# Routing steps ahead of gating on VectorE, and rows and identity scaling of the shared path on ScalarE, in a fused cross-attention and mixture-of-experts kernel

## The chip, the cores and the metric

The kernel runs on one core of a Trainium2 chip. It is one launch. The metric is device time in microseconds; the median of three runs of the kernel before is 1365.5 us (1364.32 to 1367.94).

The core has five engines with a queue each. PE is TensorE (matmul), DVE is VectorE, ACT is ScalarE, POOL is GpSimd, SP is the sync engine, which here only issues DMAs. Every engine works its own list in order and waits for the others by semaphores. An instruction that waits therefore holds up everything behind it on its engine.

## The reference

The input x has 16 batches of 256 rows of 256 numbers. First comes gated cross-attention, then a gated feed-forward part with routed experts and a shared path:

```python
x = x + tanh(g_xattn) * xattn(ctx, layernorm(x), ...)      # 16 heads of 64, keys and values from [ctx; x]
x = x + tanh(g_ffn) * ffn(layernorm(x), ...)

# ffn, h = layernorm(x), flat = its 4096 rows
probs = softmax(flat @ router_w + router_bias)             # 16 choices
top_w, top_i = top_k(probs, 2); norm_w = top_w / (sum(top_w) + 1e-6)
combine = sum(one_hot(top_i) * norm_w)
routed = combine[:, 15] * flat                             # the 16th choice is the identity
for e in range(15):
    routed += combine[:, e] * (silu(flat @ gate_w[e]) * (flat @ up_w[e]) @ down_w[e])
gate = conv1d(h, conv_w, kernel 3, causal)
shared = silu(gate) * (h @ shared_up_w) @ shared_down_w
return shared + routed
```

## The kernel before, in words

x lies in SBUF as X, 32 tiles of 128 rows (two tiles a batch). The program has three stretches.

**Attention** is a software pipeline of 128 steps (16 batches times 8 pairs of heads) with a loop in its middle. Some work belongs to step n but is done a fixed number of steps later, the lag. The routing of a batch is spread over such lags: after the attention of batch j is added to X, `route_vector` and its siblings do STATS (lag 13, mean and variance of the rows), ROWS (16, normalized rows into h_send), TURN (17 and 18, two transposes on PE), LOGITS (19), PICK (22, the two best choices), RANK (22, matmuls that count how many earlier rows chose each expert), PAGES (23), SLOTS (26, the slot number of each row, then a scatter of the rows to `slots_x` in DRAM by POOL) and SECOND (27, the same for the second choice; it rewrites h_send, so it waits until the first scatter has landed). The last batch is j = 15, so routing goes on for 20 steps after step 127. They are numbered N to N+19, with N = 128. A step N+k does whatever has the right lag there: SLOTS of batch 14 is at N+10, STATS, PICK, PAGES, SLOTS and SECOND of batch 15 are at N+5, N+14, N+15, N+18 and N+19.

**Between attention and the tiles** these 20 steps are mixed with the shared path of batches 0 to 8. `plan()` writes the order by hand, and every engine follows the same list, each doing its own part of an item. Item `("shared", i)` is: DVE makes the normalized rows of batch i+1 (`rows`, into h_row, two instructions); PE transposes the rows of batch i (below T(i)), does the convolution and the up matmul of batch i-1 and the down matmul of batch i-2; ACT copies the transposed rows to hT and takes silu of batch i-1 (act_sh). Item `("gate", i)` is DVE alone: the product gated of batch i-1, then for batch i-2 the identity scaling X = X * x_mul + x_add (two instructions), then the addition of the down result to X (two instructions). In the text, "block i" is PE's part of `("shared", i)`, and gated(m), scaling(m), adding(m) are DVE's parts for batch m. Item `("weights", ...)` turns the logits into the weights of the choices, for tiles 0 to 27 at i = 2 and for the last four after i = 8; it makes x_mul and x_add, and ACT supplies exponentials in its middle.

**The tiles**: 80 tiles of 128 rows, one expert each, are loaded from `slots_x`, and PE, ACT and DVE work on four of them at once (transpose, gate and up matmul, silu, product, transpose, down matmul, scatter by POOL). The first load waits for all scatters. The shared path of batches 9 to 15 goes on there: a block after every eighth tile, its gate after the tile that follows. From tile 26 on the results are gathered back and added to X ("sum"), and stored.

PE waits for gated(m-1) before the convolution of batch m, since both use the PSUM bank pgs, and for adding(m-1) before the down matmul of batch m. The tile's copy xT on DVE frees the PSUM area into which PE puts the next tile's transpose.

What the names are in the rows: `pj<-ident,h_row` (L483) is T(i), `pj<-hT,w_cv` and `pj<-hT,w_su` (L493, L496) convolution and up, `yb<-w_sd,gated` (L507) down; `ov<-seen,all_ones` (L994) is RANK; `ov<-ident,h_send` (L979) is TURN; `h_send<-choice` (L890) is the first instruction of SLOTS, `h_send<-h_send` (L904) of SECOND.

Of the kernel before, what the change touches and what calls it, by code (L numbers as in the profile page):

```python
# [89 lines left out]
def routing_state(nc, keep, s):  # L90
# [3 lines left out]
    def sb(name, shape, dt=F32):  # L94
        return keep.enter_context(nc.sbuf_tensor(name, shape, dt))

    def sem(name):
# [17 lines left out]
        w_top=sb("w_top", [P, NT, 2]), w_id=sb("w_id", [P, NT, 2]), x_mul=sb("x_mul", [P, NT]), x_add=sb("x_add", [P, NT]),  # L115
# [4 lines left out]
def experts(nc, c, X, ident, tanh_g, kept, att, gate_w, up_w, down_w, slots_x, routed_y, out, s):  # L120
# [78 lines left out]
    def plan():  # L199

        steps = list(range(att.N, att.last_step + 1))
        goes_along = (1, 1, 2, 1, 2, 2, 3, 4, 4)
        items = []
        for i in range(EARLY):
            for _ in range(goes_along[i]):
                items.append(("attend", steps.pop(0)))
            if i == 2:
                items.append(("weights", slice(0, WEIGHED)))
            items += [("shared", i), ("gate", i)]
        assert not steps  # L210
        items.append(("weights", slice(WEIGHED, NT)))
# [101 lines left out]
    def scalar(act, attend):  # L313
        parts = [0]

        def shared(i):
# [9 lines left out]
            if on[1]:  # L326
# [35 lines left out]
    def vector(dve, attend):  # L362
# [8 lines left out]
        def rows(b):  # L371
            if b >= 2:
                dve.wait_ge(t_full, b - 1)
            if b >= B - 2:
                dve.wait_ge(att.h_rows, b + 1)
            for t in range(QT):
                n = QT * b + t
                last = ts(h_row[:, b % 2, t, :], X[:, n, :], kept.h_mv[:, n, 0:1], kept.h_rstd[:, n:n + 1],
                          ALU.subtract, ALU.mult)
            last.then_inc(h_ready, 1)  # L380

        def shared(i):
            if i == 0:
                dve.wait_ge(att.h_rows, B - 2)
                rows(0)
            if i + 1 < B:
                rows(i + 1)

        def gate(i):
# [1097 lines left out]
```

## Time and profile before

| | |
|---|---|
| median of three runs | 1365.5 us |
| the profiled execution | 1364.59 us, of which the span of its instructions is 1362.8 us |
| PE busy | 1257.7 us, 92% |
| DVE busy | 900.1 us, 66% |
| POOL busy | 738.3 us, 54% |
| ACT busy | 636.2 us, 47% |
| granted PE clock, mean | 0.981 of full speed |

All times inside the execution are counted from the start of the span. Shares are averages: PE at 92% says that attention and most of the tiles keep it busy, and in the row of 40 slices the places where it isn't stand out. Slices 31 to 33 of PE read 8, 8, 6 (each slice is 34 us), and these hold the stretch between attention and the tiles. A line of the timeline gives the start, the duration of the group, the engine, the line of the kernel, the operation, what is written and read, the shapes and the count, and in brackets how long the engine idled before and who released it.

### The profile page before, as it was taken

The page shows a single profiled execution, that of the slowest core. Times are in us where ns is not written, and L with a number is a line of the kernel's source. Part 1 is how long each engine was busy: PE and PEld are TensorE (multiplying, and loading weights), DVE is VectorE, ACT ScalarE, POOL GpSimd, SP SyncE. Part 2 cuts the span into 40 slices and gives each one's busy share as a digit, 9 for nine tenths or more (in the row PEclk, how much of TensorE's full clock was granted, in tenths as well). Part 3 has the DMA queues.
Part 4 walks back from the last instruction along what each step waited for, and adds up shares of the span by engine and source line. Part 5 has one row for each costly group of instructions (what it writes and reads, how often), then busy time and mean ns, then how long its engine had stood idle before and what let it go on. Part 6 is the DMA issues. An engine that isn't in the chain of part 4 may idle for free. (4 is left out here: it accounts for less than half of the span.)

```text
span 1362.8 us, 28186 instructions
## 1 busy us (share of the span) xinstructions
PE 1257.7 (92%) x8982; PEld 1023.9 (75%) x8982; DVE 900.1 (66%) x2710; ACT 636.2 (47%) x1958; POOL 738.3 (54%) x894
## 2 busy tenths in 40 slices
PE   1899999999999999999999999999999886999996
PEld 1688888878787877778778878788888774877764
DVE  4566677776776777676767676777666564455464
ACT  2555555454554454555454545554555421333332
POOL 1655645666555666566565646565656412454444
PEclk9999999999999999999999999999999987999998
DMA  4950000000000000000000000000000601345656
GB/s 129 296 161 4 3 1 4 17 4 17 7 13 13 9 11 10 12 9 15 7 19 2 19 3 20 1 19 1 17 2 17 182 8 49 112 126 163 201 175 201
DMA packets 61823, 70.90 MB, mean 52 GB/s; under 512 B 7056, under 2 KB 56160, under 8 KB 61664
## 3 DMA queue, kind: packets, MB, share of 16 engines
q1 hardware_dynamic: 54464, 49.96, 12.7%
q0 software_dynamic: 6912, 18.95, 3.8%
q8 instruction: 84, 1.38, 0.4%
q14 instruction: 75, 0.61, 0.1%
q10 hardware_dynamic: 288, 0.00, 0.0%
HBM read 35.19 MB, written 33.70 MB: 51 GB/s over the span
## 5 line engine op out<-in xcount | busy, mean ns | idle before, releaser
L1087 POOL TENSOR_SCALAR probs<-probs,inv_sum 128x333 f32<-128x333 f32 x384 | 425.4, 1123 | 0.0
L1137 ACT ACTIVATE probs<-st,neg_max 128x333 f32<-128x333 f32 x512 | 268.8, 538 | 270.8 <-DVE neg_max L1276 270.8
L1084 POOL TENSOR_TENSOR probs<-probs,inv_sum 128x333 f32<-128x333 f32 x128 | 94.7, 740 | 403.4 <-DVE inv_sum L1287 403.1
L1276 DVE TENSOR_REDUCE neg_max<-st 128x2 f32<-128x666 f32 x256 | 205.9, 846 | 133.1 <-PE st L1369 133.1
L1353 PE MATMUL st<-ident,probs 128*128 128x128 f32 (+1 forms) x1536 | 204.1, 273 | 1.1 <-POOL probs L1087 1.1
L1388 PE MATMUL ov<-PT,V 128*64 128x256 f32 (+1 forms) x1536 | 197.5, 392 | 0.0
L1353 PEld LDWEIGHTS st<-ident,probs 128*128 128x128 f32 (+1 forms) x1536 | 182.8, 143 | 17.9 <-POOL probs L1087 1.4
L1323 PE MATMUL pj<-wkv,lT 128*128 128x512 f32 (+1 forms) x576 | 158.5, 411 | 16.1 <-DVE Q_hl L1296 15.9
L1369 PE MATMUL st<-K_hl,Q_hl 64*128 64x334 f32 x1536 | 153.1, 331 | 18.3 <-issue 8.9
L1308 DVE COPY PT<-st 128x512 f32<-128x512 f32 x256 | 163.8, 682 | 0.8 <-PE st L1353 0.8
L1388 PEld LDWEIGHTS ov<-PT,V 128*64 128x64 f32 (+1 forms) x1536 | 100.2, 138 | 64.7 <-issue 28.5
L1369 PEld LDWEIGHTS st<-K_hl,Q_hl 64*128 64x128 f32 x1536 | 118.8, 187 | 38.9 <-issue 23.4
L1163 ACT ACTIVATE V<-pj 128x512 f32<-128x512 f32 (+1 forms) x96 | 57.2, 596 | 194.1 <-PE pj L1323 194.1
L1323 PE MATMUL pj<-lT,wkv 128*128 128x334 f32 x768 | 140.5, 318 | 2.3 <-DVE wkv L1252 2.3
L1323 PEld LDWEIGHTS pj<-lT,wq 128*128 128x128 f32 x768 | 99.6, 190 | 53.4 <-issue 49.0
L1323 PEld LDWEIGHTS pj<-wkv,lT 128*128 128x128 f32 (+1 forms) x576 | 93.6, 175 | 50.3 <-DVE Q_hl L1296 18.7
L1323 PE MATMUL pj<-lT,wq 128*128 128x256 f32 x768 | 126.7, 300 | 4.1 <-DVE lT L1237 4.1
L1449 PE MATMUL yb<-wo,OT_hl 128*128 128x256 f32 x768 | 122.3, 295 | 0.5 <-DVE OT_hl L1291 0.5
L1323 PEld LDWEIGHTS pj<-lT,wkv 128*128 128x128 f32 x768 | 119.2, 190 | 2.6 <-DVE wkv L1252 2.6
L1137 ACT ACTIVATION_READ_ACCUMULATOR probs<-st,neg_max 128x1 f32 x512 | 103.8, 203 | 1.7 <-issue 1.6
L1449 PEld LDWEIGHTS yb<-wo,OT_hl 128*128 128x128 f32 x768 | 99.3, 190 | 0.8 <-DVE OT_hl L1291 0.8
L1168 ACT ACTIVATE PT<-st 77x512 f32<-77x512 f32 x128 | 75.1, 587 | 29.8 <-PE st L1353 29.8
(175 smaller groups left out, 1729.6 us busy)
## 6 DMA issues: line engine op xcount, KB each, us to landing
slots_x<-zeros SPq DMA_DIRECT2D x10, 1032.0 KB, 13.5
V<-slots_x SPq DMA_DIRECT2D x80, 129.0 KB
yg<-routed_y SPq DMA_DIRECT2D x32, 256.0 KB, 3.2
out<-X SPq DMA_DIRECT2D x32, 128.0 KB
stage<-in_L_xattn_Wkv SPq DMA_DIRECT2D x4, 512.0 KB, 4.0
X<-in_x SPq DMA_DIRECT2D x2, 1024.0 KB, 13.9
w_gu<-in_L_ffn_expert_gate_w SPq DMA_DIRECT2D x2, 960.0 KB, 9.3
w_gu<-in_L_ffn_expert_up_w SPq DMA_DIRECT2D x2, 960.0 KB, 10.3
```

The lines of the kernel that those rows point to most:

```text
L1084: pool.tensor_tensor(probs[:, v, 0, 0:SKV], probs[:, v, 0, 0:SKV], inv_sum[:, v, 0:1].to_broadcast([P, SKV]), ALU.mult).then_inc(normed, 1)
L1087: pool.tensor_scalar(probs[:, v, i, 0:SKV], probs[:, v, i, 0:SKV], inv_sum[:, v, i:i + 1], None, ALU.mult).then_inc(normed, 1)
L1137: nc.scalar.activation(probs[:, v, i, 0:SKV], st_bank(i)[:, 0:SKV], ACT.Exp, bias=neg_max[:, v, i:i + 1], accum_out=sums[:, v, i:i + 1]).t ...
L1163: copy(V[0:kn, kt, half * 512:(half + 1) * 512], bank[0:kn, :], ACT.Copy).then_inc(free, 1)
L1168: copy(PT[0:kn, v, 2, :], st_bank(2)[0:kn, :], ACT.Copy).then_inc(pt_hi, 1)
L1276: nc.vector.tensor_reduce(neg_max[:, v, 2 * i:2 * i + 2], st[i][:, :, 0:SKV], AX.X, ALU.max, negate=True).then_inc(maxed, 1)
L1308: nc.vector.tensor_copy(PT[:, v, kt, :], st_bank(kt)).then_inc(pt_lo, 1)
L1323: last = mm(out, lhs(a, k), rhs(r, k), start=(k == 0 and i == 0), stop=(k == KD - 1 and i == 2))
L1353: last = nc.tensor.transpose(st_bank(kt)[0:kn, at:at + P], probs[:, v, i, k0:k0 + kn], ident[:])
L1369: last = mm(st_bank(2 * qt + head)[:, 0:SKVE], Q_hl[own, r, a, qt * P:(qt + 1) * P], K_hl[own, r, a_, :], start=(n == 0), stop=(n == 2))
L1388: last = mm(ov[half * HALF:(half + 1) * HALF, 0:SQ], V[0:kn, kt, head * DH:(head + 1) * DH], PT[0:kn, v, kt, half * SQ:(half + 1) * SQ], s ...
L1449: last = mm(yb[:, t * D:(t + 1) * D], OT_hl[:, v, a, t * P:(t + 1) * P], wo[:, r_, q, :], start=(q == 0 and t == 0 and i == 0), stop=(q == ...
```

## The change

Three things change.

1. The order in `plan()`. Before, at each i, a few attention steps came first and then `("shared", i), ("gate", i)`. Now the steps from N+4 on stand between `shared` and `gate` of the same i, so that DVE does them before gated; and they are spread otherwise, so that step N+19 comes at i = 7 and no longer at i = 8. The DVE's reads of PE's results (LOGITS and RANK, now items `("reads", n)`) come after the gate. The second `weights` comes at i = 7, ahead of block 8.
2. The rows of the shared path are made by ACT, as Identity with a scale and a bias (h_rstd and the new h_shift = -mean * rstd, which DVE makes in two instructions in all).
3. The identity scaling is made by ACT, after act_sh in `("shared", i)`. The adding on DVE waits for it by the semaphore `scaled`. The chain that makes x_mul and x_add is one dependent step shorter.

```diff
     def plan():
-        steps = list(range(att.N, att.last_step + 1))
-        goes_along = (1, 1, 2, 1, 2, 2, 3, 4, 4)
+        N = att.N
+        before = {0: [N], 1: [N + 1], 2: [N + 2, N + 3]}
+        during = {2: range(N + 4, N + 7), 3: range(N + 7, N + 10), 4: range(N + 10, N + 14), 5: [N + 14],
+                  6: range(N + 15, N + 19), 7: [N + 19]}
+        reads = {2: [N + 6], 4: [N + 11], 5: [N + 14]}
         items = []
         for i in range(EARLY):
-            for _ in range(goes_along[i]):
-                items.append(("attend", steps.pop(0)))
+            items += [("attend", n) for n in before.get(i, ())]
             if i == 2:
-                items.append(("weights", slice(0, WEIGHED)))
-            items += [("shared", i), ("gate", i)]
-        items.append(("weights", slice(WEIGHED, NT)))
+                items += [("reads", N + 3), ("weights", slice(0, WEIGHED))]
+            items.append(("shared", i))
+            items += [("attend", n) for n in during.get(i, ())]
+            items.append(("gate", i))
+            items += [("reads", n) for n in reads.get(i, ())]
+            if i == 7:
+                items.append(("weights", slice(WEIGHED, NT)))
...
     def scalar(act, attend):
+        def rows(b):
+            if b >= 2:
+                act.wait_ge(t_full, b - 1)
+            act.wait_ge(shift_ready, 1 if QT * b < WEIGHED else 2)
+            for t in range(QT):
+                n = QT * b + t
+                last = nc.scalar.activation(h_row[:, b % 2, t, :], X[:, n, :], ACT.Identity,
+                                            bias=h_shift[:, n:n + 1], scale=kept.h_rstd[:, n:n + 1])
+            last.then_inc(h_ready, 1)
         def shared(i):
+            if i == 0:
+                rows(0)
+            if i + 1 < B:
+                rows(i + 1)
...
+            if on[2]:
+                m = i - 2
+                act.wait_ge(mul_ready, 1 if QT * m < WEIGHED else 2)
+                for t in range(QT):
+                    n = QT * m + t
+                    last = nc.scalar.activation(X[:, n, :], X[:, n, :], ACT.Identity,
+                                                bias=x_add[:, n:n + 1], scale=x_mul[:, n:n + 1])
+                last.then_inc(scaled, 1)
...
     def vector(dve, attend):
-        def rows(b):
-            ...
-                last = ts(h_row[:, b % 2, t, :], X[:, n, :], kept.h_mv[:, n, 0:1], kept.h_rstd[:, n:n + 1],
-                          ALU.subtract, ALU.mult)
+        def shift(tl):
+            dve.wait_ge(att.h_rows, tl.stop // QT)
+            dve.wait_ge(att.y_read, tl.stop // QT)
+            nc.vector.scalar_tensor_tensor(h_shift[:, tl], kept.h_mv[:, tl, 0], -1.0, kept.h_rstd[:, tl],
+                                           ALU.mult, ALU.mult).then_inc(shift_ready, 1)
         def gate(i):
...
                 m = i - 2
-                for t in range(QT):
-                    n = QT * m + t
-                    last = ts(X[:, n, :], X[:, n, :], x_mul[:, n:n + 1], x_add[:, n:n + 1], ALU.mult, ALU.add)
-                last.then_inc(scaled, 1)
                 dve.wait_ge(down_full, m + 1)
                 dve.wait_ge(scaled, m + 1)
...
         def weights(tl):
+            if tl.start:
+                shift(tl)
...
-            then(tt(x_add[:, tl], x_add[:, tl], kept.h_rstd[:, tl], ALU.mult))
-            ts(x_mul[:, tl], x_add[:, tl], 1.0, None, ALU.add)
-            then(tt(x_add[:, tl], x_add[:, tl], kept.h_mv[:, tl, 0], ALU.mult))
-            then(ts(x_add[:, tl], x_add[:, tl], -1.0, None, ALU.mult))
+            then(nc.vector.tensor_tensor(x_mul[:, tl], x_add[:, tl], kept.h_rstd[:, tl], ALU.mult))
+            tt(x_add[:, tl], x_add[:, tl], h_shift[:, tl], ALU.mult)
+            ts(x_mul[:, tl], x_mul[:, tl], 1.0, None, ALU.add).then_inc(mul_ready, 1)
```

How the instructions stand on their engines, at three places. The first is DVE behind the first `weights` (i = 2). Before:

```order
L435 TENSOR_SCALAR x_add<-x_add 128x28
L378 TENSOR_SCALAR h_row<-X,h_mv,h_rstd 128x256 x2
L396 TENSOR_TENSOR gated<-pj,act_sh 128x256
L401 TENSOR_SCALAR X<-X,x_mul,x_add 128x256 x2
L407 SCALAR_TENSOR_TENSOR X<-yb,tanh_g,X 128x256 x2
L378 TENSOR_SCALAR h_row<-X,h_mv,h_rstd 128x256 x2
L396 TENSOR_TENSOR gated<-pj,act_sh 128x256
L401 TENSOR_SCALAR X<-X,x_mul,x_add 128x256 x2
L407 SCALAR_TENSOR_TENSOR X<-yb,tanh_g,X 128x256 x2
L820 MEMSET route_carrier 128x1
L829 BN_STATS h_stats<-X 128x6 x2
```

And in the changed kernel, where STATS of batch 15 and PICK of batch 14 follow the weights at once:

```order
L455 TENSOR_SCALAR x_mul<-x_mul 128x28
L840 MEMSET route_carrier 128x1
L849 BN_STATS h_stats<-X 128x6 x2
L840 MEMSET route_carrier 128x1
L853 BN_AGGR h_now<-h_stats 128x2 x2
L840 MEMSET route_carrier 128x1
L875 MAX top<-logit 128x8 x2
```

Two gates stood before STATS and now none does; gated(1) comes eleven rows further down, after PICK. On PE the matmuls of RANK moved likewise, from behind block 3 to behind block 2.

The second place is DVE at SLOTS of batch 15. Before, it came after the gate of i = 7, at i = 8:

```order
L884 TENSOR_TENSOR place<-ranks,room 128x32
L378 TENSOR_SCALAR h_row<-X,h_mv,h_rstd 128x256 x2
L396 TENSOR_TENSOR gated<-pj,act_sh 128x256
L401 TENSOR_SCALAR X<-X,x_mul,x_add 128x256 x2
L407 SCALAR_TENSOR_TENSOR X<-yb,tanh_g,X 128x256 x2
L890 TENSOR_SCALAR h_send<-choice 128x2
L891 TENSOR_TENSOR place<-place,grown 128x32
```

And in the changed kernel, at i = 6:

```order
L904 TENSOR_TENSOR place<-ranks,room 128x32
L910 TENSOR_SCALAR h_send<-choice 128x2
L911 TENSOR_TENSOR place<-place,grown 128x32
L912 TENSOR_TENSOR place<-place,ranks 128x32
L913 TENSOR_TENSOR place<-place,base 128x32
L914 TENSOR_TENSOR placed<-hot,place 128x64
L915 TENSOR_REDUCE slot_f<-placed 128x4
L916 CAST slot_i<-slot_f 128x4
```

SLOTS follows PAGES (which ends with `place<-ranks,room`) without a gate between them, and the gate of i = 6 comes behind SLOTS.

The third place is ACT around the second exponentials. Before, they were its last work ahead of the tiles:

```order
L324 ACTIVATE hT<-pj 128x2x256
L331 ACTIVATE act_sh<-pj 128x256
L336 ACT_TABLE_LOAD
L336 ACTIVATE ex<-ex 128x64
L337 ACTIVATE e<-e 128x4
L346 ACT_TABLE_LOAD
L346 ACTIVATE act_e<-st 128x128 x2
```

And in the changed kernel:

```order
L360 ACTIVATE X<-X,x_add,x_mul 128x256 x2
L367 ACT_TABLE_LOAD
L367 ACTIVATE ex<-ex 128x64
L368 ACTIVATE e<-e 128x4
L331 ACTIVATE h_row<-X,h_shift,h_rstd 128x256 x2
L347 ACTIVATE hT<-pj 128x2x256
L354 ACT_TABLE_LOAD
L354 ACTIVATE act_sh<-pj 128x256
L360 ACTIVATE X<-X,x_add,x_mul 128x256 x2
L377 ACTIVATE act_e<-st 128x128 x2
```

A whole `shared` item, with the rows, the copy to hT, the reload of the silu table, act_sh and the scaling, now stands between the exponentials and the first tile's silu.

## Rows read from the trace of the kernel before

**Rows 1.** From attention's end to the first tile: stretch, length, busy PE, PEld, DVE, ACT, POOL, clock.
```profile
1073.19:1155.78 82.59, 61.41 (x276) 50.59 (x277) 44.24 (x196) 18.58 (x33) 17.11 (x23) 0.80 0.24 71
```

**Rows 2.** Timeline of DVE, from the end of the first weights to the first tile.
```profile
1095.93 0.74 DVE L378 TENSOR_SCALAR h_row<-X,h_mv,h_rstd 128x256 f32<-128x256 f32 x2
...
1103.79 0.42 DVE L829 BATCH_NORM_STATS2 h_stats<-X 128x6 f32<-128x256 f32 x1
...
1114.77 0.42 DVE L396 TENSOR_TENSOR gated<-pj,act_sh 128x256 f32<-128x256 f32 x1 [5.59 <-ACT act_sh L331]
...
1134.15 0.21 DVE L920 COPY ranks<-ov 128x48 f32<-128x48 f32 x1 [1.45 <-PE ov L998]
...
1136.04 0.73 DVE L378 TENSOR_SCALAR h_row<-X,h_mv,h_rstd 128x256 f32<-128x256 f32 x2
...
1143.30 0.16 DVE L890 TENSOR_SCALAR h_send<-choice 128x2 int32<-128x2 f32 x1
...
1148.97 0.17 DVE L904 TENSOR_SCALAR h_send<-h_send 128x2 f32<-128x2 f32 x1 [3.88 <-DMA slots_x<-h_send,slot_i]
...
1151.73 0.15 DVE L419 TENSOR_TENSOR e<-best 128x4 f32<-128x4 f32 x1
...
1156.55 0.42 DVE L443 COPY xT<-st 128x256 f32<-128x256 f32 x1 [1.60 <-PE st L530]
```

**Rows 3.** Timeline of PE in the same stretch.
```profile
1097.30 0.60 PE L483 MATMUL pj<-ident,h_row 128*128 128x128 f32 x4
...
1106.82 0.64 PE L994 MATMUL ov<-seen,all_ones 128*128 128x32 f32 x2 [4.60 <-DVE seen L869]
...
1108.13 1.09 PE L483 MATMUL pj<-ident,h_row 128*128 128x128 f32 x4
...
1115.02 0.60 PE L483 MATMUL pj<-ident,h_row 128*128 128x128 f32 x4
...
1119.78 0.38 PE L979 MATMUL ov<-ident,h_send 128*128 128x128 f32 x2
1120.63 0.44 PE L979 MATMUL ov<-ident,h_send 128*128 128x128 f32 x2 [0.47 <-ACT h_turned L967]
...
1122.46 0.93 PE L483 MATMUL pj<-ident,h_row 128*128 128x128 f32 x4
...
1155.78 0.66 PE L530 MATMUL st<-ident,V 128*128 128x128 f32 x2 [9.29 <-DMA V<-slots_x]
```

**Rows 4.** Busy time in stretches of 5 us; the number after POOL is PE's clock.
```profile
1105.00:1110.00 5.00, 3.18 (x13) 3.00 (x14) 2.41 (x16) 0.60 (x1) 0.82 (x2) 0.56 0.01 3
...
1115.00:1120.00 5.00, 5.00 (x27) 4.32 (x25) 4.64 (x22) 0.98 (x2) 0.00 (x0) 1.00 0.01 2
```

**Rows 5.** Timeline of ACT: copy to hT, table load, exponential of the last tiles.
```profile
1142.21 0.60 ACT L324 ACTIVATE hT<-pj 128x512 f32<-128x512 f32 x1 [0.92 <-PE pj L483]
...
1146.07 1.28 ACT L336 ACT_TABLE_LOAD   x1
1152.05 0.26 ACT L336 ACTIVATE ex<-ex 128x64 f32<-128x64 f32 x1 [4.70 <-DVE ex L420]
```

**Rows 6.** Groups of ACT by shape, first 60 us: a source in SBUF.
```profile
L1125 ACT ACTIVATE wkv<-stage 128x1024 fp32r<-128x1024 f32 x4 | 4.2, 1056 | 13.8 <-DMA stage<-in_L_xattn_Wkv 13.8
```

**Rows 7.** Timeline of all engines around a gate among the tiles.
```profile
1173.16 0.38 ACT L331 ACTIVATE act_sh<-pj 128x256 f32<-128x256 f32 x1 [2.86 <-PE pj L496]
...
1175.11 0.28 ACT L346 ACTIVATE act_e<-st 128x128 f32<-128x128 f32 x1 [1.56 <-PE st L540]
...
1175.96 0.72 DVE L401 TENSOR_SCALAR X<-X,x_mul,x_add 128x256 f32<-128x256 f32 x2
...
1176.79 0.88 DVE L407 SCALAR_TENSOR_TENSOR X<-yb,tanh_g,X 128x256 f32<-128x256 f32 x2
...
1177.58 0.41 DVE L443 COPY xT<-st 128x256 f32<-128x256 f32 x1
...
1178.14 0.41 PE L530 MATMUL st<-ident,V 128*128 128x128 f32 x2 [0.90 <-DVE xT L443]
```

**Rows 8.** Who waited for whom among the tiles: us in total, times, longest.
```profile
PE st L530 <- DVE xT L443: 13.0, 22, 0.9
```

More of the change, by code:

```diff
@@ L114, in routing_state @@
         z_sum=sb("z_sum", [P, NT]), e2=sb("e2", [P, NT]), den=sb("den", [P, NT]),
-        w_top=sb("w_top", [P, NT, 2]), w_id=sb("w_id", [P, NT, 2]), x_mul=sb("x_mul", [P, NT]), x_add=sb("x_add", [P, NT]),
+        w_top=sb("w_top", [P, NT, 2]), w_id=sb("w_id", [P, NT, 2]), x_mul=sb("x_mul", [P, NT]), x_add=sb("x_add", [P, NT]), h_shift=sb("h_shift", [P, NT]),
         conv_in=sem("conv_in"), misc_in=sem("misc_in"), route_consts=sem("route_consts"), cv_ready=sem("cv_ready"),
@@ L156, in experts @@
     x_add = kept.x_add
+    h_shift = kept.h_shift
     pts, pgs, pys = att.pj[0], att.pj[1], att.yb
@@ L175, in experts @@
     scaled = sem("scaled")
+    shift_ready = sem("shift_ready")
+    mul_ready = sem("mul_ready")
     carried = sem("carried")
@@ L199, in plan @@
     def plan():
-        steps = list(range(att.N, att.last_step + 1))
-        goes_along = (1, 1, 2, 1, 2, 2, 3, 4, 4)
+        N = att.N
[3 more added lines that the diff above has]
+        reads = {2: [N + 6], 4: [N + 11], 5: [N + 14]}
         items = []
         for i in range(EARLY):
-            for _ in range(goes_along[i]):
-                items.append(("attend", steps.pop(0)))
+            items += [("attend", n) for n in before.get(i, ())]
             if i == 2:
-                items.append(("weights", slice(0, WEIGHED)))
-            items += [("shared", i), ("gate", i)]
-        assert not steps
-        items.append(("weights", slice(WEIGHED, NT)))
+                items += [("reads", N + 3), ("weights", slice(0, WEIGHED))]
[5 more added lines that the diff above has]
+                items.append(("weights", slice(WEIGHED, NT)))
+        assert att.last_step == N + 19
         shared = EARLY
@@ L369, in then @@
             dve.wait_ge(weigh, steps[0])
-        def rows(b):
[L372 to L375, printed above, removed]
-            for t in range(QT):
-                n = QT * b + t
-                last = ts(h_row[:, b % 2, t, :], X[:, n, :], kept.h_mv[:, n, 0:1], kept.h_rstd[:, n:n + 1],
-                          ALU.subtract, ALU.mult)
-            last.then_inc(h_ready, 1)
         def shared(i):
             if i == 0:
[L384 to L387, printed above, removed]
+                shift(slice(0, WEIGHED))
+        def shift(tl):
[3 more added lines that the diff above has]
+                                           ALU.mult, ALU.mult).then_inc(shift_ready, 1)
         def gate(i):
@@ L398, in gate @@
                 m = i - 2
-                for t in range(QT):
-                    n = QT * m + t
-                    last = ts(X[:, n, :], X[:, n, :], x_mul[:, n:n + 1], x_add[:, n:n + 1], ALU.mult, ALU.add)
-                last.then_inc(scaled, 1)
                 dve.wait_ge(down_full, m + 1)
@@ L466, in combine @@
                 add(t, 1).then_inc(final, 1)
-        follow(attend, {"shared": shared, "gate": gate, "weights": weights, "tile": tile, "sum": combine})
+        follow(attend, {"shared": shared, "gate": gate, "weights": weights, "reads": lambda n: att.vector_reads(dve, n), "tile": tile, "sum": combine})
     def tensor(pe, attend):
@@ L1311, in step @@
                 split_rows(bb, u // PAIRS + 1, L_STEPS[p], (u // PAIRS + 1) % 2)
-            route_vector_reads(dve, bb, u, has)
+            if has(0):
+                route_vector_reads(dve, bb, u, has)
         return pipeline(dve, step)
```

5 lines of the change are left out of this document (4 added, 1 removed).

## The prediction

> **What bounds the kernel now.** I read the slices of busy time first (where is PE not full), then the chain that ended last, then busy time by stretch, and last the timelines of single engines where the chain leaves PE.
>
> The change touches nothing before the end of attention, at 1073.2. From there to the first tile's matmul at 1155.78 PE is busy 61.4 of 82.6 us at a mean clock of 0.80 [rows 1]. PE sat idle 9.29 us before it, for a load of rows that wait for the last scatter [rows 3]. So routing of batch 15 ends the stretch. The reader is to see that routing is slow only because of its place in DVE's queue: DVE waits 5.59 us for act_sh in one gate [rows 2], with routing steps queued behind. RANK waits for PICK that way and PE idles 4.60 us [rows 3], after which its clock is at 0.56, against 1.00 further on [rows 4]. These two are its levels, 1.2 GHz and 2.4 GHz (0.56 mixes them). A block (transpose, convolution, up, down) takes 1108.13 to 1115.02 = 6.9 us mostly at the lower one and 1115.02 to 1119.78 = 4.76 us at the higher one [rows 3].
>
> Among the tiles PE waits for xT 22 times, 13.0 us in all, at most 0.9 [rows 8]. One 0.90 stands behind a gate on DVE: gated, scaling, adding, then xT [rows 7].
>
> **The stretch before the tiles, walked through with the new order.** Attention's tail stays. The first rows are now made by ACT behind one h_shift on DVE. An ACT instruction of 128x256 takes 0.38 [rows 7], and one of 1024 columns out of SBUF 1.056 [rows 6], so source SBUF is no dearer; I take 0.8 for a pair. DVE's pair takes 0.74 or a little more [rows 2], so T(0) starts within 0.3 of before. I count 0.
>
> *i = 2.* The weights end at 1095.93 [rows 2]; one dependent step less, so 1095.7. STATS and PICK come next at once: 1103.79 to RANK at 1106.82 = 3.03 [rows 2, 3]. RANK starts at 1098.75. PE was ready at 1097.30 (where T(3) starts now), so it idles 1.4. RANK takes 1106.82 to 1108.13 = 1.3 [rows 3]: T(3) at 1100.05, later than before by 2.75, paid here for what follows.
>
> *i = 3.* PE idled, so I take the lower clock: block 3 ends at 1106.95. gated can start 0.25 before a block ends (1114.77 against 1115.02) [rows 2, 3]. Then ACT scales (0.8), the adding waits for that and takes 0.8 (1176.79 to 1177.58) [rows 7]: DVE is free 1.35 after a block's end, at 1108.3. PAGES and ROWS ran before in its wait for act_sh, which hides them.
>
> *i = 4.* SLOTS to SECOND took 1143.30 to 1148.97 = 5.67, most of it the scatter [rows 2]: SECOND of batch 14 at 1113.95. It stands before gated(3) now. That is an added wait: behind it are gated(3), on which the convolution in block 5 waits, and adding(2). PE meanwhile has one transpose of TURN (0.4), block 4 at the higher clock (to 1112.15), then the other transpose and LOGITS, 1120.63 to 1122.46 = 1.8 [rows 3], so T(5) at 1113.95 and its convolution at 1114.7. gated(3) ends at 1114.5. The scatter is just hidden; each us more would cost one.
>
> *i = 5, 6.* Block 5 follows a small gap and tiny matmuls; I take 6.9 again: 1120.85. RANK 1.3: T(6) at 1122.15. DVE is free at 1122.2, PAGES 1134.15 to 1136.04 = 1.9 [rows 2], SLOTS of batch 15 at 1124.1 instead of 1143.30, SECOND at 1129.75 instead of 1148.97. From SECOND to the first tile was 6.81 [rows 2, 3]: 1136.55 is when the data allows a tile.
>
> *i = 6 to 8.* Three blocks at the higher clock from 1122.15: 1126.9, 1131.7, 1136.45. PE and data thus arrive together, and what is late next is DVE and ACT. The last adding of i = 7 ends at 1133.05, h_shift and the differences are ready at 1133.55 (0.2 for one, an estimate by the 1.9 of PAGES' nine instructions; 0.3 for the other, 1151.73 to 1152.05 [rows 2, 5]), two exponentials 0.4, rows 0.8, the copy to hT 0.6, the silu table 1.28 [rows 5]: act_sh(7) at 1136.65, 0.85 later than PE would allow. gated 0.4 [rows 2], scaling 0.8, adding 0.8: xT of tile 0 at 1138.65. It was at 1156.55 [rows 2]. **Gain 17.9 us.**
>
> What follows a table load is the least known price here: the row shows 1.28 for the load itself [rows 5] and nothing queued directly behind it. The page "ScalarE: Activation LUTs" of the Trainium skill, section "What ACT_TABLE_LOAD costs", says that a switch costs about 1.38 us of drain on top, which speaks against this change. By that rule the gain of this stretch would be 16.5 in place of 17.9; my sum goes by the row.
>
> **The tiles.** DVE loses two things. The rows cost nothing before, since DVE made them while PE was in the block; on ACT they lie beside the block too. The scaling did cost: adding started 1176.79 - 1175.96 = 0.83 later through it, xT with it, and PE idled 0.90 for xT [rows 7]. Now ACT has act_sh at 1173.16 to 1173.54, the scaling to 1174.35, and its next work, act_e, can't start before 1175.11 [rows 7]. So it is hidden, and done 1.6 before DVE came to the scaling (1175.96) [rows 7]; `scaled` isn't waited for. If this cover went, each gate would cost up to 0.8. PE's idle falls from 0.90 to 0.07, and the next limit is PE's own order. I take 0.8 for each of 8 gates (those of batches 7 to 14 for the scaling) and 0.5 for the last, which has less PE work beside it: **6.9 us**. Bounds: 0, if something else is late at once, and 0.83 x 9 = 7.5.
>
> **Sum.** 17.9 + 6.9 = 24.8. The profiled execution took 1364.59 (span 1362.8), so 1339.8. The median stands 0.9 above that execution: **1340.7 us**.
>
> **Bounds of the walk.** The clock decides most. A block at the other level is 2.1 away: if blocks 3 and 5 both ran at the higher one, 4.2 less; if 6 and 7 also ran at the lower one, 4.2 more. The wait for the scatter in front of gating was seen as 5.67. ACT's pair may cost 0.76 to 1.1 (0.38 twice, or 1.056 for one long instruction): up to 0.3 at each of some five places on the path, 1.5. The likeliest case's own range is thus 1335 to 1346.
>
> **Rivals.**
> 1. *The clock stays up.* The idle of 1.4 before RANK is short against the 4.60 that stood there. For: the smaller gap. Against: the row of TURN shows idle of only 0.47 and still 0.93 for T(6) behind it, against 0.60 at the higher clock [rows 3]. The walk is 4.2 shorter, and the tiles start at most 1.5 faster: 1335 to 1336.
> 2. *Work behind the silu table starts late.* Before, each load had idle time behind it; now act_sh(7) is queued behind one and on the path. If the start is late by as much again as the load is long, 1.3 more: 1342.0. For: the trace can't exclude it; against: no row shows it. That is the mechanism of the rule above.
> 3. *The path moves to ACT and its handoffs.* Every gate waits for act_sh and then for the scaling, and T and the convolution wait for rows and hT from the same queue. If PE loses 0.8, one pair, at each of blocks 3 to 8: 4.8 more, 1345.5. Against: rows are made a block ahead.
> 4. *The tiles gain nothing*, since PE then waits for another: 6.9 more, 1347.6. For: the 13 other waits for xT, (13.0 - 9 x 0.9) / 13 = 0.4 each [rows 8], stand where DVE is busy without a gate; against: the idle of 0.90 behind a gate names DVE as releaser [rows 7].
> 5. *The other side: SECOND in front of gating.* Scatters that landed late would stall DVE at i = 4 and i = 7, and with it gated, PE and the clock. Up to 5.7 us from SLOTS to SECOND it is hidden. Every us beyond costs one in each of the two places, and a block at the lower clock 2.1 each. The change is slower than before once 2 x (t - 5.7) + 4.2 exceeds 24.8, that is, when t is over 16 us. At t = 20 the time is 1340.7 + 28.6 + 4.2 = 1373.5. Against: 5.67 measured, and the queues are nearly empty there (DMA share 0.01 in the stretches shown [rows 4]).
> 6. *The change doesn't shorten routing*, if DVE, not its waits, were the limit: then only the tiles gain, 1358.6. Against: DVE is busy 44.2 of 82.6 us [rows 1].
>
> **How the numbers follow.** Chances: my forecast 0.42, rival 1 0.16, rival 2 0.12, rival 3 0.11, rival 4 0.10, rival 5 0.03, rival 6 0.03, and 0.03 that all evens out to within what can be told. This kernel's measurement tells 0.3%, about 4 us, from no change. All cases but the fifth and the last lie below 1361.4, so faster 0.94, same 0.03, slower 0.03. The range for 8 in 10 takes in the forecast's own range, rival 1, and rivals 2 to 4 with a margin for a clock that falls once more: 1332 to 1351.
>
> **What would show it.** In the profile of the changed kernel: idle of PE before the first tile falls from 9.29 to about 1; the first tile's xT stands at 1137 to 1140; SLOTS of batch 15 at 1124, SECOND 5.7 later, with gated behind it; PE idles about 1.4 before the first RANK between attention and tiles, and under 0.5 before the second; DVE is idle for ACT before each adding by 0.3 to 0.5 ahead of the tiles, and not at all among them; the 0.90 waits for xT behind a gate shrink to 0.1. Wrong would be: a first tile later than 1145 (then rival 3, 5 or 6, told apart by who releases gated), waits for xT as long as before (rival 4), act_sh more than 1 us behind the silu table (rival 2), or idle of PE for gated.

## The result, and the profile after

On one chip, four runs of each: before 1366.42 us, after 1343.83 us (1342.28 to 1344.31), ratio 0.983, 95% interval 0.982 to 0.985. That is faster by 22.6 us, where 24.8 were forecast; 1340.7 was predicted, so the median is 3.1 above the forecast and within the range. Another set of runs with the same kernel, told below, gave the same ratio.

The profiled execution took 1342.28 us (span 1340.5). Busy time from attention's end to the first tile's matmul, in the columns of [rows 1], and two stretches of 5 us as in [rows 4]:

```profile
1074.17:1139.84 65.67, 55.05 (x276) 45.62 (x277) 31.40 (x161) 34.62 (x67) 16.81 (x23) 0.90 0.31 90
1100.00:1105.00 5.00, 5.00 (x17) 4.40 (x18) 3.47 (x18) 0.60 (x1) 0.00 (x0) 0.50 0.02 3
...
1115.00:1120.00 5.00, 4.45 (x17) 3.61 (x17) 3.25 (x22) 0.98 (x2) 2.13 (x3) 0.66 0.18 63
```

The stretch is 65.67 us long, not 82.59. PE had 276 instructions before and has 276 now, but they take 55.05 instead of 61.41 us, for the mean clock is 0.90 instead of 0.80. So 6.4 us of the 16.9 are busy time, at the same count of matmuls and a higher clock, and 10.6 are idle time that went. DVE has 35 instructions less, ACT 34 more. In the second row the clock (0.50) is at the lower of its two levels (1.2 GHz), in the third (0.66) it is so for part of the time.

PE in the same stretch, as in [rows 3]. T is the group L503, a block's convolution L513:

```profile
1073.06 0.97 PE L1470 MATMUL yb<-wo,OT_hl 128*128 128x256 f32 x6 [0.53 <-DVE OT_hl L1311]
...
1090.90 2.76 PE L513 MATMUL pj<-hT,w_cv 128*128 128x256 f32 x12
...
1099.85 0.64 PE L1014 MATMUL ov<-seen,all_ones 128*128 128x32 f32 x2 [4.47 <-DVE seen L889]
...
1101.15 1.09 PE L503 MATMUL pj<-ident,h_row 128*128 128x128 f32 x4
1102.04 4.86 PE L513 MATMUL pj<-hT,w_cv 128*128 128x256 f32 x12
...
1114.46 1.06 PE L1007 MATMUL ov<-w_rt,h_turned 128*128 128x16 f32 x8 [0.64 <-issue]
1115.37 0.63 PE L503 MATMUL pj<-ident,h_row 128*128 128x128 f32 x4
1116.56 4.50 PE L513 MATMUL pj<-hT,w_cv 128*128 128x256 f32 x12 [0.55 <-DVE gated L419]
...
1123.21 0.64 PE L503 MATMUL pj<-ident,h_row 128*128 128x128 f32 x4
...
1139.84 0.41 PE L550 MATMUL st<-ident,V 128*128 128x128 f32 x2 [2.01 <-DMA V<-slots_x]
```

Idle in front of the first tile fell from 9.29 [rows 3] to 2.01, still for the load of rows behind the last scatter. The same twelve convolution matmuls take 2.76 where the granted clock is 1.00 (the one at 1090.90), 4.50 where it is 0.61 on average and 4.86 where it is 0.56, that is, where part of the group ran at the lower level.

DVE, as in [rows 2]. L419 is gated, L426 the adding, L910 the first instruction of SLOTS, L924 the first of SECOND; the line of POOL is the issue of the first of the two scatters of batch 15:

```profile
1108.22 0.42 DVE L419 TENSOR_TENSOR gated<-pj,act_sh 128x256 f32<-128x256 f32 x1 [4.02 <-ACT act_sh L354]
...
1109.28 0.88 DVE L426 SCALAR_TENSOR_TENSOR X<-yb,tanh_g,X 128x256 f32<-128x256 f32 x2 [0.63 <-ACT X L360]
1110.07 0.16 DVE L910 TENSOR_SCALAR h_send<-choice 128x2 int32<-128x2 f32 x1
1115.85 0.17 DVE L924 TENSOR_SCALAR h_send<-h_send 128x2 f32<-128x2 f32 x1 [3.99 <-DMA slots_x<-h_send,slot_i]
1116.00 0.42 DVE L419 TENSOR_TENSOR gated<-pj,act_sh 128x256 f32<-128x256 f32 x1
...
1122.37 0.42 DVE L419 TENSOR_TENSOR gated<-pj,act_sh 128x256 f32<-128x256 f32 x1 [3.01 <-ACT act_sh L354]
...
1126.09 0.17 DVE L910 TENSOR_SCALAR h_send<-choice 128x2 int32<-128x2 f32 x1
...
1127.95 0.98 POOL L977 DMA_INDIRECT slots_x<-h_send,slot_i  x1 [0.15 <-POOL pool_route L975]
...
1132.57 0.17 DVE L924 TENSOR_SCALAR h_send<-h_send 128x2 f32<-128x2 f32 x1 [2.88 <-DMA slots_x<-h_send,slot_i]
...
1138.44 0.42 DVE L419 TENSOR_TENSOR gated<-pj,act_sh 128x256 f32<-128x256 f32 x1 [0.83 <-ACT act_sh L354]
1139.50 0.88 DVE L426 SCALAR_TENSOR_TENSOR X<-yb,tanh_g,X 128x256 f32<-128x256 f32 x2 [0.63 <-ACT X L360]
1140.29 0.42 DVE L463 COPY xT<-st 128x256 f32<-128x256 f32 x1
```

SLOTS of batch 15 stands at 1126.09, where it was at 1143.30 [rows 2]: routing did go ahead of gating. Of the waits for act_sh, 4.02 is left ahead of gated(2), 3.01 ahead of gated(4) and 0.83 ahead of gated(7). SECOND waits 3.99 for the scatter with gated(3) behind it, and PE then waits 0.55 for that gated. At the end both paths meet: xT starts without idle after the adding, and 0.45 after the tile's transpose, which is what xT also takes behind it when DVE is free (below, rows on VectorE).

ACT around the two table loads, as in [rows 5], and its two new instructions (groups by shape: count, busy us, mean ns):

```profile
1133.61 1.28 ACT L367 ACT_TABLE_LOAD   x1
1134.90 0.26 ACT L367 ACTIVATE ex<-ex 128x64 f32<-128x64 f32 x1
...
1136.73 1.28 ACT L354 ACT_TABLE_LOAD   x1
1138.03 0.38 ACT L354 ACTIVATE act_sh<-pj 128x256 f32<-128x256 f32 x1
```

```profile
L360 ACT ACTIVATE X<-X,x_add,x_mul 128x256 f32<-128x256 f32 x32 | 17.3, 589 | 0.1
L331 ACT ACTIVATE h_row<-X,h_shift,h_rstd 128x256 f32<-128x256 f32 x32 | 17.2, 589 | 1.2 <-DVE h_shift L409 1.2
...
L354 ACT ACTIVATE act_sh<-pj 128x256 f32<-128x256 f32 x16 | 6.1, 383 | 36.2 <-PE pj L516 36.2
```

act_sh starts 0.02 after the load's end. And each of the two new instructions of 128x256 takes 589 ns, where act_sh takes 383.

Among the tiles, around a gate, as in [rows 7], and who waited for whom there, as in [rows 8]:

```profile
1156.85 0.38 ACT L354 ACTIVATE act_sh<-pj 128x256 f32<-128x256 f32 x1 [2.05 <-PE pj L516]
1157.13 1.08 ACT L360 ACTIVATE X<-X,x_add,x_mul 128x256 f32<-128x256 f32 x2
...
1158.80 0.28 ACT L377 ACTIVATE act_e<-st 128x128 f32<-128x128 f32 x1 [0.59 <-PE st L560]
...
1159.31 0.41 DVE L419 TENSOR_TENSOR gated<-pj,act_sh 128x256 f32<-128x256 f32 x1
...
1159.64 0.87 DVE L426 SCALAR_TENSOR_TENSOR X<-yb,tanh_g,X 128x256 f32<-128x256 f32 x2
...
1160.43 0.41 DVE L463 COPY xT<-st 128x256 f32<-128x256 f32 x1
...
1160.99 0.41 PE L550 MATMUL st<-ident,V 128*128 128x128 f32 x2
```

```profile
PE st L550 <- issue: 4.4, 10, 0.6
...
PE st L550 <- DVE xT L463: 0.6, 1, 0.6
```

The scaling is over at 1158.21, before act_e and 1.4 before the adding. PE goes on without the 0.90 of [rows 7]. In place of 22 waits for xT, 13.0 us in all [rows 8], 11 gaps are left, 5.0 in all: one of 0.6 at the first tile, and ten of 0.16 to 0.57 without a releaser in sight, none of them where the eight waits of 0.90 behind a gate had stood. DVE waits for ACT before no adding among the tiles.

**Where the time went.** I measure from one row that both traces have, the last output projection of attention's step N (`yb<-wo` of six matmuls after 0.53 idle): 1072.13 before, 1073.06 after.

| us | before | after | difference |
|---|---|---|---|
| start to that row | 1072.13 | 1073.06 | +0.93 |
| from it to the first tile's xT | 84.42 | 67.23 | -17.19 |
| from there to the end of the span | 206.25 | 200.21 | -6.04 |
| span | 1362.8 | 1340.5 | -22.3 |

The first line moves between traces of kernels that are alike up to there: 1072.1 to 1075.8 over all that are told here. So lengths of the stretch are counted from that row.

### The profile page after: what moved, and what is told of

It is laid out like the page before. It is cut to its first block, busy times and chain, and to the rows that moved or that the text cites. A ratio compares the mean times of both kernels' runs of the same rounds, so it can differ in the third digit from the quotient of the medians.

```text
span 1340.5 us, 28196 instructions
## 1 busy us (share of the span) xinstructions
PE 1251.8 (93%) x8982; PEld 1018.9 (76%) x8982; DVE 877.1 (65%) x2646; ACT 665.2 (50%) x2022; POOL 739.4 (55%) x894
## 3 DMA queue, kind: packets, MB, share of 16 engines
q8 instruction: 84, 1.38, 0.4%
## 4 chain that ended last, share of the span: by engine, by line
PE 39%; POOL 28%; issue 23%; DVE 5%; DMA 3%; ACT 2%; POOLq 0%; SPq 0%; DVEq 0%; ACTq 0%
POOL probs L1107 19%; PE pj L1344 9%; PE st L560 6%; PE ov L1409 4%; PE st L1390 4%; PE st L1374 3%; POOL probs L1104 3%; POOL slots_x L977 3%; PE pj L513 3%; PE ov L579 3%; PE yb L1470 2%; PE st L550 2%; POOL rstd L1087 1%; DMA slots_x<-h_send,slot_i 1%; DVE PT L1328 1%
## 6 DMA issues: line engine op xcount, KB each, us to landing
w_gu<-in_L_ffn_expert_up_w SPq DMA_DIRECT2D x2, 960.0 KB, 10.2
```

## The experiments

Experiments 1 to 4 ran on one chip and 5 to 8 on another, each set beside the kernel before (1365.03 and 1365.48 us). A time in us is the median, a ratio is against the kernel before, with its 95% interval.

**1. The order alone (e_order).** The plan of the change, with rows and scaling back on DVE and the chain that makes x_mul and x_add as before:

```diff
+        def rows(b):                       # on DVE, from shared(i)
+                last = ts(h_row[:, b % 2, t, :], X[:, n, :], kept.h_mv[:, n, 0:1], kept.h_rstd[:, n:n + 1],
+                          ALU.subtract, ALU.mult)
...
+                    last = ts(X[:, n, :], X[:, n, :], x_mul[:, n:n + 1], x_add[:, n:n + 1], ALU.mult, ALU.add)
```

> Only the new order of plan(); rows and identity scaling stay on DVE as in the kernel before. Theory: the order is what shortens the stretch before the tiles, and DVE has room for rows (0.74 a block) and scaling (0.83) beside the waits for act_sh. The stretch from the last attention step to the first tile's xT is 16.5 to 18 us shorter than before, the tiles take as long as before (206 us from that xT to the end), 1348 to 1350 us. Rival: the order needs the work taken off DVE, since routing now stands in front of gated: then the stretch gains under 12 us and the time is 1354 or more.

1350.92, ratio 0.989 (0.986 to 0.991). From the row above to xT 1145.03 - 1074.16 = 70.87, 13.6 less than before; from there to the end 205.9, 0.4 less. So the order makes most of the first part and next to nothing among the tiles. The expectation of 16.5 to 18 and 1348 to 1350 was missed, and so was the rival's (under 12, 1354 or more): the stretch is 3.6 us short of order and operations together. PE and DVE show where a part of it went:

```profile
1119.36 5.46 PE L502 MATMUL pj<-hT,w_cv 128*128 128x256 f32 x12 [1.83 <-DVE gated L405]
```

```profile
1112.52 0.16 DVE L899 TENSOR_SCALAR h_send<-choice 128x2 int32<-128x2 f32 x1
...
1118.64 0.17 DVE L913 TENSOR_SCALAR h_send<-h_send 128x2 f32<-128x2 f32 x1 [4.32 <-DMA slots_x<-h_send,slot_i]
```

DVE had a scaling (1110.24) and rows (1111.88) to do in front of SLOTS of batch 14. Counted from the common row SLOTS came 1.35 later than in the change, SECOND followed after 6.12 instead of 5.78, and gated(3) stands right behind it. So the convolution waited 1.83, not 0.55, and was slow (granted clock 0.50) for the whole of its 5.46 us. At the end xT came 0.87 after the tile's transpose would allow it (1145.03 against 1143.71 + 0.45), behind gated, scaling and adding on DVE.

**2. The operations alone (e_ops).** The plan of before, rows and scaling on ACT:

```diff
+        steps = list(range(att.N, att.last_step + 1))
+        goes_along = (1, 1, 2, 1, 2, 2, 3, 4, 4)
...
+            items += [("shared", i), ("gate", i)]
```

> Only rows and identity scaling on ACT; plan() as in the kernel before. Theory: in the stretch before the tiles the routing still waits behind the gates, so it changes by 0 to -2 us; among the tiles each gate saves 0.7 to 0.8, 6.3 in all; 1358 to 1361 us. The waits of PE for xT of 0.90 behind a gate fall to about 0.1. Rival: ACT's pair (0.98 from start to start with what follows) is waited for among the tiles too, or PE meets another limit: tiles as before, 1365 or more.

1359.11, ratio 0.995 (0.993 to 0.997): the time is as expected. Among the tiles it is 5.2 less than before (xT to the end takes 201.1), where 6.3 were expected, and the idle before the first tile stays at 9.10:

```profile
1155.61 0.66 PE L544 MATMUL st<-ident,V 128*128 128x128 f32 x2 [9.10 <-DMA V<-slots_x]
```

That SECOND of batch 15 stands at 1148.84 (before: 1148.97) is in part chance: in this trace the common row came at 1075.78, 3.65 later, and the stretch from it to xT is 3.9 shorter (80.53), where 0 to 2 were expected. PE ran attention's tail and the convolution of block 2 (2.76 against 5.08) at a higher clock.

Order (0.989) times operations (0.995) is 0.984; the change is 0.983. By part, the two bring 13.6 + 3.9 = 17.5 in the stretch (the change: 17.2) and 0.4 + 5.2 = 5.6 among the tiles (6.0). So they add up as far as these runs can tell: the medians give 14.1 + 5.9 = 20.0 of 22.6 us, and each interval is about 3 us to either side.

**3. Rows back on VectorE (e_rows_dve).** The change, with only the rows of the shared batches on DVE:

```diff
-            for t in range(QT):            # on ACT
-                last = nc.scalar.activation(h_row[:, b % 2, t, :], X[:, n, :], ACT.Identity,
-                                            bias=h_shift[:, n:n + 1], scale=kept.h_rstd[:, n:n + 1])
+                last = ts(h_row[:, b % 2, t, :], X[:, n, :], kept.h_mv[:, n, 0:1], kept.h_rstd[:, n:n + 1],
+                          ALU.subtract, ALU.mult)
```

> The changed kernel with the rows back on DVE; scaling stays on ACT. Theory: the rows on ACT bring nothing (they lie beside the block on either engine) and cost at T(0) and at the last act_sh before the tiles; the first tile's data sets the start anyway, so the time is within 1 us of the changed kernel, 1343 to 1345. Rival: taking the rows off DVE is part of the gain, 0.7 at each of blocks 3 to 8 and at eight gates: 1348 or more.

1340.68, ratio 0.982 (0.981 to 0.984). That is below the 1343 to 1345 of the theory and far from the rival's 1348, and the interval overlaps that of the change. No gain from the rows' move to ACT is to be seen; from xT to the end this trace takes 200.3, as the change does (200.2), so the gain among the tiles is the scaling's. PE and DVE of this run:

```profile
1115.93 2.83 PE L513 MATMUL pj<-hT,w_cv 128*128 128x256 f32 x12 [1.21 <-DVE gated L419]
...
1137.76 0.41 PE L550 MATMUL st<-ident,V 128*128 128x128 f32 x2 [1.53 <-DMA V<-slots_x]
```

```profile
1138.20 0.42 DVE L463 COPY xT<-st 128x256 f32<-128x256 f32 x1 [0.45 <-PE st L550]
```

Its convolution waited 1.21, longer than the 0.55 of the change, and yet ran at the higher clock (granted 1.00). So the length of that one idle time does not decide the level by itself. PE's clock is one reason in sight why this run is rather the faster one: attention's tail took 6.93 from the common row to batch 0's convolution against 8.82 in the change, and the convolution of block 5 took 2.83 against 4.50.

From experiment 1 this run differs by the scaling and the shorter chain, and it is 10.2 us faster, more than the 5.9 of experiment 2: 5.6 among the tiles, 6.5 in the stretch. Of the 6.5, 4.2 are PE's clock in attention's tail (8.50 to 6.93) and in that convolution (5.46 to 2.83). Whether the scaling's place causes this higher clock was not tried.

**4. SECOND behind gating (e_second_behind).** The wait that the plan put in front of gated(3) and gated(6) goes behind them:

```diff
-        during = {2: range(N + 4, N + 7), 3: range(N + 7, N + 10), 4: range(N + 10, N + 14), 5: [N + 14],
-                  6: range(N + 15, N + 19), 7: [N + 19]}
+        during = {2: range(N + 4, N + 7), 3: range(N + 7, N + 10), 4: [N + 10], 5: [N + 14],
+                  6: range(N + 15, N + 19)}
+        behind = {4: range(N + 11, N + 14), 7: [N + 19]}
```

> The changed kernel with SECOND (and what goes with it) behind the gate at i = 4 and at i = 7 instead of ahead of it. Theory: at i = 4 PE's wait of 0.55 for gated goes; at i = 7 SECOND of batch 15 comes 1.6 later (behind adding, which waits for ACT), and as the tiles start when its scatter has been loaded, the first tile starts 1 to 1.6 later: 1344.3 to 1345.5 us. Rival: SECOND ahead of gating is what costs, so it gets faster: 1342 to 1343.

1341.3, ratio 0.982 (0.980 to 0.984): not slower. My expectation was wrong. Of what the early gated brings it counted only the 0.55 of the wait, and not the 1.74 of the convolution at the higher clock. PE in the same place has no wait, and its granted clock is 1.00:

```profile
1115.88 2.76 PE L515 MATMUL pj<-hT,w_cv 128*128 128x256 f32 x12
...
1138.80 0.41 PE L552 MATMUL st<-ident,V 128*128 128x128 f32 x2 [3.40 <-DMA V<-slots_x]
```

SLOTS of batch 15 came at 1123.67, 2.4 before that of the change; SECOND, now queued behind gated(6) and its adding, came 8.40 after it instead of 6.48, at 1132.07, 0.5 before that of the change. What one wait brought, the other nearly took.

**5. The change once more (after_again)**, unchanged, beside the three that follow.

> The changed kernel itself, beside the others of this call on the same chip, so that a difference of 3 us between it and a variant can be told. Every theory: 1342 to 1345 us, ratio to the kernel before 0.982 to 0.985. If it comes at 1340 or below, rows on VectorE (1340.7) and SECOND behind gating (1341.3) were no faster than the change, and the gain of 0 to 3 us read for them was the chip's.

1342.88 (1337.53 to 1343.61), ratio 0.983 (0.981 to 0.984). One of five runs took 1337.5: single runs of one kernel lie up to 6 us apart. The medians of experiments 3 and 4 lie 2 to 3 us from those of the change with overlapping intervals, on another chip than this run, so I read no gain or loss from them.

**6. Another plan (e_plan2).** Two waits are taken out of the path of batch 15: gate(2) goes ahead of STATS and PICK, RANK one block back, and SECOND of batch 14 behind gate(4):

```diff
-        during = {2: range(N + 4, N + 7), 3: range(N + 7, N + 10), 4: range(N + 10, N + 14), 5: [N + 14],
-                  6: range(N + 15, N + 19), 7: [N + 19]}
-        reads = {2: [N + 6], 4: [N + 11], 5: [N + 14]}
+        during = {3: range(N + 4, N + 7), 4: range(N + 7, N + 11), 5: [N + 14], 6: range(N + 15, N + 19), 7: [N + 19]}
+        behind = {4: range(N + 11, N + 14)}
+        reads = {3: [N + 6], 4: [N + 11], 5: [N + 14]}
```

> The plan alone is changed again: gate(2) stands ahead of STATS and PICK (RANK(14) on TensorE one block later), SECOND(14) stands behind gate(4). Theory (the two waits that the change's plan adds or leaves on the path, VectorE for act_sh at i=2 (4.02 us) and for the scatter in front of gated(3), delay batch 15): DVE is free for SLOTS(15) earlier, at 1118 to 1121 instead of 1126.1, the first xT stands at 1133 to 1136 instead of 1140.3, the time is 1337 to 1340 us. Rival (TensorE and its clock set the end, since every block of shared work must still be done before the tiles): SLOTS(15) comes earlier but the blocks 6 to 8 end as late as now, first xT at 1139 to 1141, time 1341 to 1345, same as the change. Which of the two it is shows in what the first tile's matmul waited for: a DMA (data) or its own queue.

1334.14 (1334.03 to 1336.06), ratio 0.978 (0.976 to 0.979): below the change's interval, the fastest of all, and 3 us below the 1337 to 1340 of the theory. PE and DVE:

```profile
1099.56 0.41 PE L1015 MATMUL ov<-seen,all_ones 128*128 128x32 f32 x2
...
1108.36 4.44 PE L514 MATMUL pj<-hT,w_cv 128*128 128x256 f32 x12
...
1131.23 0.41 PE L551 MATMUL st<-ident,V 128*128 128x128 f32 x2 [1.67 <-DMA V<-slots_x]
```

```profile
1117.84 0.17 DVE L911 TENSOR_SCALAR h_send<-choice 128x2 int32<-128x2 f32 x1
...
1123.48 0.17 DVE L925 TENSOR_SCALAR h_send<-h_send 128x2 f32<-128x2 f32 x1 [2.04 <-DMA slots_x<-h_send,slot_i]
...
1131.26 0.88 DVE L427 SCALAR_TENSOR_TENSOR X<-yb,tanh_g,X 128x256 f32<-128x256 f32 x2 [0.63 <-ACT X L361]
1132.05 0.42 DVE L464 COPY xT<-st 128x256 f32<-128x256 f32 x1
```

RANK stands at 1099.56 with no idle before it, SLOTS of batch 15 at 1117.84, and from the common row to xT it is 1132.05 - 1072.28 = 59.77, against 67.34 in the trace of experiment 5. PE still waits for data before the first tile, so the rival (the time stays as it was, since blocks 6 to 8 end as late as before) is out. The first xT starts behind the adding, 0.4 after the tile's transpose would allow it (1131.23 + 0.45): ACT's chain of handoffs is here the last to end, by that much, as it is in the trace of experiment 5 (1140.92 against 1140.10 + 0.45). Of the 7.6 us, 1.6 are no merit of the plan as far as can be seen: right after T(0) attention's tail ran at the higher clock here and partly at the lower in experiment 5 (7.18 against 8.79 from the common row to batch 0's convolution). The rest, 6.0, lies within the 4 to 7 that the theory had given from xT to xT (1140.3 to 1133 or 1136). It too holds clock: RANK has no idle of over 4 us before it any more, and the convolution of block 3 takes 2.83 against 4.93, while that of block 2 takes 3.96 against 2.76. The two waits were taken out together; what each is worth was not tried.

**7. That plan with rows on VectorE (e_plan2_rows_dve)**: the edits of 3 and 6 together.

> The same plan, and the rows of shared batches back on VectorE (the scaling stays on ScalarE). Theory of ScalarE's handoffs (a pair of 128x256 takes 1.08 us on ScalarE, 0.74 on VectorE, and act_sh, the scaling and the rows stand in one queue): 1 to 3 us less than the same plan with rows on ScalarE, 1335 to 1339. Rival (VectorE is the engine that ends the stretch with this plan): 8 pairs of 0.74 more in front of SLOTS(15) cost 1 to 3 us, 1340 to 1343.

1336.51, ratio 0.978 (0.977 to 0.980): the same as 6 by the intervals. It lies in the theory's 1335 to 1339 but not below experiment 6, as the theory had it, and the rival's 1340 did not come. Where the rows are made makes no difference that these runs can tell, but the two places cost in different spots. On DVE the rows of batch 3 stand behind the first weights, and T(3) waits for them:

```profile
1096.69 0.66 PE L504 MATMUL pj<-ident,h_row 128*128 128x128 f32 x4 [2.22 <-DVE h_row L396]
```

**8. What an instruction on ScalarE costs (e_form).** One run, of a kernel that leaves out the row scale and the identity scaling.

```diff
                 last = nc.scalar.activation(h_row[:, b % 2, t, :], X[:, n, :], ACT.Identity,
-                                            bias=h_shift[:, n:n + 1], scale=kept.h_rstd[:, n:n + 1])
+                                            bias=h_shift[:, n:n + 1])
...
-                    last = nc.scalar.activation(X[:, n, :], X[:, n, :], ACT.Identity,
-                                                bias=x_add[:, n:n + 1], scale=x_mul[:, n:n + 1])
+                    last = nc.scalar.activation(X[:, n, :], X[:, n, :], ACT.Copy)
```

> Leaves out the row scale of the shared rows (Identity with a bias per partition only) and the whole identity scaling (a plain Copy in its place). One look, for the price of ScalarE's 128x256 instruction: 589 ns with scale and bias per partition from SBUF, 383 ns for the copy of 128x256 out of PSUM. Theory A (the two operands per partition cost it): Copy takes about 0.38, bias alone between. Theory B (source and target in SBUF cost it): all forms stay at 0.58 to 0.60. Time: by A some 1 to 2 us below the change, by B the same as the change.

```profile
L331 ACT ACTIVATE h_row<-X,h_shift 128x256 f32<-128x256 f32 x32 | 14.3, 498 | 1.2 <-DVE h_shift L408 1.2
...
L360 ACT ACTIVATE X<-X 128x256 f32<-128x256 f32 x32 | 11.4, 408 | 0.3 <-DVE x_mul L454 0.3
```

A plain copy out of SBUF takes 408, with a bias per partition 498, with bias and scale 589. So each operand per partition costs 90 ns, and the copy out of SBUF costs only 25 more than an instruction of 128x256 out of PSUM (383): theory A. The run took 1335.0, 7.9 below the change's median of the same set. Shorter instructions alone were expected to give 1 to 2; this run also had the higher clock in attention's tail (7.01 from the common row to batch 0's convolution, against 8.79) and in block 5 (2.83 against 4.51), 3.5 us together, and a lower one in block 2 (4.19 against 2.76); and it is one run.

## Why the prediction was right, and where it was off

The walk's times are set against the trace by the 0.93 by which attention's common row came later:

| step | walk + 0.93 | trace |
|---|---|---|
| RANK of batch 14 | 1099.7 | 1099.85 |
| T(3) | 1101.0 | 1101.15 |
| SECOND of batch 14 | 1114.9 | 1115.85 |
| T(5) | 1114.9 | 1115.37 |
| T(6) | 1123.1 | 1123.21 |
| SLOTS of batch 15 | 1125.0 | 1126.09 |
| SECOND of batch 15 | 1130.7 | 1132.57 |
| data for the first tile | 1137.5 | 1139.84 |
| act_sh(7) | 1137.6 | 1138.03 |
| xT of the first tile | 1139.6 | 1140.29 |

**The mechanism** held, and experiments 1 to 3 show its parts apart: the order alone brings 13.6 where the change brings 17.2 in the stretch, and the scaling nearly all of what is won among the tiles. That so many rows of the walk agree within 0.5 is in part luck, since errors cancelled: RANK came on time although PE idled three times as long as said, and T(6) came on time because block 5 ended 0.84 after the walk while the second RANK took 0.6 instead of 1.3.

**The miss** of 3.1 in the median is 2.5 in the profiled execution and 0.6 in the step from it to the median (1.55, where 0.9 was taken). The 2.5 are 0.93 before the change begins (nothing of it was predicted), 0.71 in the stretch, 0.86 among the tiles.

- *ACT's pair at 0.8.* This term was mis-sized: 0.98 from start to start and 1.08 to its end, near the upper bound. It was taken from an instruction without operands per partition (0.38); experiment 8 shows that these two make the price. It stands in the five waits of DVE before an adding ahead of the tiles, 0.45 to 0.63, where 0.3 to 0.5 was forecast.
- *The scatter just hidden.* It was as long as taken for batch 14 (5.78 from SLOTS to SECOND) but gated(3) came 0.55 late for the convolution: "idle of PE for gated", which the prediction had named as a sign of being wrong, did come once. For batch 15 it was 6.48, and from SECOND to the tile 7.27 (walk: 5.67 and 6.81). These 1.3 us, and SLOTS 1.1 late (block 5 ended 0.84 after the walk, the adding behind it another 0.24), are why data came 2.4 after the walk, and why PE idled 2.0 before the first tile and not about 1. In the walk the path through act_sh ended 1.65 after the data allowed (1138.65 against 1136.55 + 0.45), and that slack hid most of it: xT came only 0.7 late, 0.45 of it at act_sh(7) and 0.26 by the longer pair.
- *The idle before RANK at 1.4* was 4.47, yet RANK came when forecast. PE was ready earlier, since block 2 ran at the higher clock (2.76 where it took 5.08 before). The term cost nothing, as PE was not what was waited for.
- *The clock.* Blocks 3 and 5 mostly low, 4, 6, 7 and 8 high, as walked, and again so in experiment 5. For block 5 this was no safe call: in experiment 3, with the same plan, and in experiment 4 its convolution ran at the higher level. Rival 1 (the clock stays up; its numbers add up to 1335.0 to 1336.5, not to 1336) came in neither, since the one in block 3 stayed mostly low (4.09 and 4.74).
- *Work behind the silu table* (rival 2). act_sh started 0.02 behind the load, the exponential after the other table's load 1134.90 - (1133.61 + 1.28) = 0.01. (That other load was not in the walk; it ended at 1134.89, when DVE's differences had just been ready at 1134.85, so it cost nothing to speak of.) The 1.38 us of drain on top that the Trainium skill gives (page "ScalarE: Activation LUTs", section "What ACT_TABLE_LOAD costs") is not there in this trace; the measurement decides.
- *0.8 for each of 8 gates, 0.5 for the last.* 6.04 came instead of 6.9, that is 0.67 for each of nine. This term was sized from one gate. The scaling is hidden as said and all eight waits of 0.90 are gone (rival 4 had counted nine), but from block to block the tiles gain 0.84, 0.72, 0.77, 0.66, 0.81, 0.47 and 0.65, and 1.06 behind the last block. The small gaps of PE, most of them ahead of the blocks, stay much as they were (0.53 at 1225.37 before and at 1206.71 after). Where the rest of each 0.90 goes stays open.
- *Rivals 3 to 6.* Rival 3 (ACT's handoffs on the path) was half true at one place, gated(7) and its adding in front of the first xT: as late as the data in this trace, 0.37 later in that of experiment 5. Rival 4 fell by the 6.04. Rival 5's wait exists, 3.99 and 2.88 us long, and costs PE 0.55; that it costs block 5 its clock too is argued from experiment 4 alone, and experiment 3 speaks against it. Rival 6 fell by SLOTS, 17.2 us earlier.

## What to carry to other kernels

When a queue holds a wait for another engine in front of a long chain (routing, scatter, load), move the chain ahead, and then ask which waits the new order itself put on the chain: taking two of those out brought about 6 us more in a pair of traces here, a part of it by PE's clock. An operation moved to another engine gains only what it stood in front of; the scaling stood before xT and brought 5 to 6 us among the tiles, the rows stood beside a block and brought nothing that could be told. Take the price of the moved operation from a row with the same operands, not only the same shape.

## What was not expected of the hardware

- ScalarE's 128x256 takes 408 ns as a copy in SBUF, 498 with a bias per partition and 589 with bias and scale; with a source in PSUM and no such operands it takes 383.
- PE's granted clock fell to its lower level after idle times of less than a us each (0.64 and 0.55 before the convolution of 4.50 us; 0.64 and 0.47 before that of 4.44 us), but stayed at 1.00 after 0.64 and 1.21 (experiment 3) and after 1.53 (block 3 of experiment 2). A convolution is worth 1.7 to 2.7 us by it. Which one is hit changes from run to run of the experiments, and what decides it stays open.
- From the first instruction of SLOTS to SECOND it took 5.6 to 6.6 us (5.64, 5.78, 6.48, and 1130.96 - 1124.32 = 6.64 with rows on VectorE). The first 1.86 of that go by before POOL issues the first scatter. From this issue to SECOND it was 3.8 to 3.9 for batch 14 in the changed kernel and for batch 15 in experiment 6, and 1132.57 - 1127.95 = 4.62 for batch 15 in the changed kernel (4.78 in experiment 3). What the longer ones stood behind was not tried.
